# The first cross attention in four rounds a head instead of two, with SyncE's transfers laid out by quarters

## The reference, cut to what matters

```
q = qkv.reshape(bs * 16, ch, length)            # 16 heads, ch 16, length 512
k = v = y.reshape(bs * 16, ch, -1)              # 8192 keys
weight = einsum('bct,bcs->bts', q * scale, k * scale)
weight = softmax(weight.astype(float32), axis=-1)
a = einsum('bts,bcs->bct', weight, v)
x = x + a.reshape(bs, -1, length)
```

## Time and profile before

| | us |
|---|---|
| median of 3 runs (lowest, highest) | 1447.28 (1446.05, 1448.35) |
| the profiled execution, its own time | 1461.28 |
| its span, first to last instruction | 1459.5 |
| first cross attention in the span | 0 to about 701.8 |
| two negmax reductions in the steady part, one round apart | 297.53 and 317.35 |
| half clock in the stage, as granted in the trace | from 644.2 to 681.7 |
| mean granted TensorE clock | 0.982 |

### The profile page before, as it was taken

One profiled execution on the slowest core, in us unless ns is written; L12 is line 12 of the kernel. 1 busy time (PEld: TensorE's weight loads), 2 busy tenths in 40 slices (PEclk: granted clock), 3 DMA queues, 4 the chain that ended last, 5 costly groups with the idle time before them and its releaser, 6 DMA issues. The chain is left out here.

```text
span 1459.5 us, 27413 instructions
## 1 busy us (share of the span) xinstructions
PE 1398.2 (96%) x10740; PEld 847.7 (58%) x10740; DVE 1154.7 (79%) x1672; ACT 945.0 (65%) x1770; POOL 138.2 (9%) x171
## 2 busy tenths in 40 slices
PE   3999999999999999999899899999989889999998
PEld 2433333333333333333457899999978664568998
DVE  5999999999999999984587566666658447887665
ACT  1588888888888888876284455545533631785553
POOL 4122222212111222110000000000000000000000
PEclk9999999999999999986999999999999999999999
DMA  7644665554555444462204645554445523104540
GB/s 176 146 109 99 167 151 123 120 142 108 123 122 114 113 110 96 79 93 40 87 1 181 238 174 180 198 182 172 173 172 246 231 103 128 66 1 159 191 177 37
DMA packets 46338, 194.50 MB, mean 133 GB/s; under 512 B 16985, under 2 KB 17409, under 8 KB 34177
## 3 DMA queue, kind: packets, MB, share of 16 engines
q1 hardware_dynamic: 46032, 192.77, 44.9%
q10 hardware_dynamic: 192, 0.20, 0.1%
HBM read 167.69 MB, written 21.83 MB: 130 GB/s over the span
## 5 line engine op out<-in xcount | busy, mean ns | idle before, releaser
L526 DVE TENSOR_REDUCE pm<-bank 128x1 f32<-128x1024 f32 x512 | 621.2, 1221 | 24.6 <-PE bank L607 19.1
L585 ACT ACTIVATE probs<-bank 128x512 f32<-128x512 f32 x1024 | 554.6, 598 | 112.3 <-PE bank L626 105.1
L607 PE MATMUL bank<-kst,qst 48*128 48x512 f32 x1024 | 375.1, 457 | 22.1 <-DMA qst<-qsplit 20.4
L626 PE MATMUL bank<-qst,kst 52*128 52x512 f32 (+1 forms) x1024 | 378.6, 458 | 2.9 <-DMA qst<-nscratch 2.0
L643 PE MATMUL bank<-probs,vext 128*32 128x256 f32 x3968 | 324.8, 400 | 0.0
L626 PEld LDWEIGHTS bank<-qst,kst 52*128 52x128 f32 (+1 forms) x1024 | 155.0, 189 | 219.2 <-ACT probs L585 188.5
L1292 PE MATMUL bank<-e_xhi,e_hi 128*128 128x256 f32 (+1 forms) x784 | 223.5, 285 | 5.0 <-DVE e_lo L1227 4.5
L1292 PE MATMUL bank<-e_xhi,e_lo 128*128 128x256 f32 (+1 forms) x784 | 223.2, 285 | 0.0
L1292 PE MATMUL bank<-e_xlo,e_hi 128*128 128x256 f32 (+1 forms) x784 | 223.2, 285 | 0.0
L643 PEld LDWEIGHTS bank<-probs,vext 128*32 128x32 f32 x3968 | 79.0, 109 | 185.7 <-issue 96.3
L607 PEld LDWEIGHTS bank<-kst,qst 48*128 48x128 f32 x1024 | 151.5, 189 | 29.6 <-DMA qst<-qsplit 20.4
(11 more groups left out here) (220 smaller groups left out, 1521.0 us busy)
## 6 DMA issues: line engine op xcount, KB each, us to landing
raw<-wall SPq DMA_DIRECT2D x34, 1536.0 KB, 6.6
kst<-kscratch SPq DMA_DIRECT2D x192, 128.0 KB, 4.5
raw<-wall SPq DMA_DIRECT2D x10, 2304.0 KB, 8.5
kscratch<-ksplit SPq DMA_DIRECT2D x15, 1024.0 KB, 4.6
kraw<-ctx_rows SPq DMA_DIRECT2D x16, 512.0 KB, 6.3
vraw<-ctx_vt SPq DMA_DIRECT2D x16, 512.0 KB, 7.2
ctxT<-ctxT SPq DMA_DIRECT2D x8, 1024.0 KB, 11.6
nat<-ctx_chunks SPq DMA_DIRECT2D x6, 1024.0 KB, 21.6
```

What stands on the lines that cost most here:

```text
L526: nc.vector.tensor_reduce(pm[:, h % 2, r % 4, c:c + 1], bank[:, 2 * (r % 2):2 * (r % 2) + 2, :], AX.XY, ALU.max).then_inc(pre_reduced, 1)
L585: nc.scalar.activation(probs[:, (XST * k + n) % PR, :], bank[:, S_BANK[k][n], :], ACT.Exp, scale=XSCALE).then_inc(probs_ready, 1)
L607: ins = nc.tensor.matmul(bank[:, 2 * (r % 2) + j, :], qst[64 * j:64 * j + KR, h, tt * P:tt * P + P], kst[64 * j:64 * j + KR, h % 2, c * 51 ...
L626: nc.tensor.matmul(bank[:, S_BANK[k][n], :], kst[64 * j:64 * j + rows, h % 2, m * P:m * P + P], qst[64 * j:64 * j + rows, h, :], start=Tru ...
```

## The change

`NS` becomes 4: 64 rounds of 16 tiles, 8 iterations and 4 groups of values each. LAGP, FIRST_V and V_SCORE stay. The maximum of a round is the running one over the head's parts so far, so each round but the first of a head has a weight, three for a head instead of one. The total of a head is kept in `osb[:, 0]`: for every later round GpSimd multiplies it by the weight and adds the copied sum of the round. ScalarE copies after every round. SyncE's list is written anew for the four parts. The weights of the next stage come in eight transfers instead of four.

```
-NS = 2
+NS = 4
+W_AT = 2 * (XP + 4 - LAGP)
+    def later(k):
+        return k // NS * (NS - 1) + k % NS
 # SyncE (loads of the last heads left out)
+            for t in range(XN):
+                h, part = divmod(t, NS)
+                if t > 0:
+                    stack_negmax(t - 1)
+                if part == 0:
+                    if h < XH - 1:
+                        store_split(h + 1)
...
+                if part == 1:
+                    if h < XH - 1:
+                        load_stack(h + 1, 0)
...
+                    if 0 < h < XH - 3:
+                        sp.wait_ge(split_step, 2 * h + 4)
+                        load_raw(h + 3)
+                    if h > 0:
+                        sp.wait_ge(o_summed, (NS - 1) * h)
+                        sp.dma_start(oscratch[h - 1], osb[:, 1 + (h - 1) % 2, :]).then_inc(o_stored[(h - 1) % 2], 16)
+                if part == 2:
+                    if h < XH - 1:
+                        load_stack(h + 1, 1)
...
+                if part == 3:
+                    if h < XH - 1:
+                        load_q(h + 1)
...
+                    if h < XH - 2:
+                        sp.wait_ge(v_ready, h + 1)
+                        load_v(h + 2)
+                if t > 0 and (t - 1) % NS > 0:
+                    store_weight(t - 1)
+                    spread_weight(t - 1)
+
             stack_negmax(XN - 1)
             for h in range(XHA // 2, XHA):
                 load_nd(h)
+            store_weight(XN - 1)
+            spread_weight(XN - 1)
 # GpSimd
+            def weigh(k):
+                n = later(k)
+                pool.wait_ge(weight_moved, 32 * n)
+                if k % NS == 1:
+                    pool.wait_ge(o_copied, k)
+                else:
+                    pool.wait_ge(o_summed, n - 1)
+                total = osb[:, 0, :].rearrange("p (t c) -> p c t", t=4)
+                nc.gpsimd.tensor_tensor(total, total, weights[:, :, :], ALU.mult).then_inc(weighted, 1)
+            def sum_o(k):
+                h, part = divmod(k, NS)
+                pool.wait_ge(weighted, later(k))
+                pool.wait_ge(o_copied, k + 1)
+                to = osb[:, 0 if part < NS - 1 else 1 + h % 2, :]
+                nc.gpsimd.tensor_tensor(to, osb[:, 1 + h % 2, :], osb[:, 0, :], ALU.add).then_inc(o_summed, 1)
+            for k in range(XN):
+                h, part = divmod(k + 1, NS)
+                split_negmax(k)
+                if k % NS > 0:
+                    if later(k) > 2:
+                        pool.wait_ge(weight_ready, later(k) - 2)
+                    nc.gpsimd.tensor_tensor(mdiff[:, later(k) % 2, :], negmax[:, k % 4, :], negmax[:, (k - 1) % 4, :], ALU.subtract).then_inc(apart, 1)
+                if k > 0 and (k - 1) % NS > 0:
+                    weigh(k - 1)
+                    sum_o(k - 1)
+                if part == 1 and h < XH - 2:
                     split(h + 2)
+                if part == 1 and h == XH - 1:
                     ...   # the two memsets of nd
+                if part == 2 and h < XH - 1:
                     values(h + 1)
 # ScalarE: copy_o(k) after every round; the weight
+                    if n == W_AT and (k + 1) % NS > 0:
+                        act.wait_ge(apart, later(k + 1))
+                        if later(k + 1) > 1:
+                            act.wait_ge(weight_moved, 32 * (later(k + 1) - 1))
 # TensorE: pre waits for the keys of a head's first half in part 0, of the second half in part 2
-            for part of w_attn0: one transfer of 1024 KB
+            for part and half of w_attn0: one transfer of 512 KB
```

More of the change, by code:

```diff
@@ L315, in load_stack @@
                 if h >= 2:
-                    sp.wait_ge(scores, XST * (NS * (h - 2) + half + 1))
+                    sp.wait_ge(scores, XST * (NS * (h - 2) + NS // 2 * (half + 1)))
                 for rows in K_ROWS:
@@ L363, in _ @@
             sp.wait_ge(qsplit_ready, 4)
[L365 to L409, removed]
@@ L449, in _ @@
             nc.gpsimd.memset(marks[:, :, :].bitcast(F32), 1.0).then_inc(const_set, 1)
-            pool.wait_ge(const_set, 1)
-            nc.gpsimd.memset(marks[0:2, 1, :].bitcast(F32), 0.0).then_inc(const_set, 1)
+            for part in range(1, NS):
+                pool.wait_ge(const_set, part)
+                nc.gpsimd.memset(marks[0:2 * part, part, :].bitcast(F32), 0.0).then_inc(const_set, 1)
             nc.gpsimd.tensor_copy(g.identb[:, :], ident[:, :]).then_inc(g.ident_ready, 1)
@@ L467, in split_negmax @@
                                         ALU.subtract).then_inc(nsplit_step, 1)
[L469 to L480, removed]
@@ L482, in _ @@
-            for h in range(XH):
-                split_negmax(NS * h)
-                if h < XH - 2:
+            def weigh(k):
+                n = later(k)
+                pool.wait_ge(weight_moved, 32 * n)
+                if k % NS == 1:
+                    pool.wait_ge(o_copied, k)
+                else:
+                    pool.wait_ge(o_summed, n - 1)
+                total = osb[:, 0, :].rearrange("p (t c) -> p c t", t=4)
+                nc.gpsimd.tensor_tensor(total, total, weights[:, :, :], ALU.mult).then_inc(weighted, 1)
@@ L491, in _ @@
                     pool.wait_ge(nd_set, 2)
[L492 to L495, removed]
+                if part == 2 and h < XH - 1:
                     values(h + 1)
-                split_negmax(NS * h + 1)
-                nc.gpsimd.tensor_tensor(mdiff[:, h % 2, :], negmax[:, (NS * h + 1) % 4, :], negmax[:, NS * h % 4, :], ALU.subtract).then_inc(apart, 1)
-            weigh(XH - 1)
+            weigh(XN - 1)
         @block.vector
@@ L524, in _ @@
                     dve.wait_ge(pre_scores, XP * k + r + 1)
-                    c = 4 * half + r // 4
+                    c = 8 // NS * half + r // 4
                     nc.vector.tensor_reduce(pm[:, h % 2, r % 4, c:c + 1], bank[:, 2 * (r % 2):2 * (r % 2) + 2, :],
@@ L529, in _ @@
                 if k >= 4:
-                    dve.wait_ge(apart, (k - 4) // NS + 1)
-                nc.vector.tensor_reduce(negmax[:, k % 4, :], pm[:, h % 2, :, 0:4 * half + 4], AX.X, ALU.max, negate=True).then_inc(negmax_ready, 1)
+                    dve.wait_ge(apart, later(k - 3))
+                nc.vector.tensor_reduce(negmax[:, k % 4, :], pm[:, h % 2, :, 0:8 // NS * (half + 1)], AX.X, ALU.max, negate=True).then_inc(negmax_ready, 1)
             turn_negmax(XN - 1)
@@ L560, in copy_o @@
             def copy_o(k):
-                h, half = divmod(k, NS)
+                h, part = divmod(k, NS)
                 act.wait_ge(pv_done, XG * (k + 1))
-                if half == 0 and h > 0:
-                    act.wait_ge(o_summed, h)
-                if half == 1 and h >= 2:
+                if part == 0 and h > 0:
+                    act.wait_ge(o_summed, (NS - 1) * h)
+                if part == 1 and h >= 2:
                     act.wait_ge(o_stored[h % 2], h // 2 * 16)
-                nc.scalar.copy(osb[:, 0 if half == 0 else 1 + h % 2, :], bank[:, V_BANK[k], :]).then_inc(o_copied, 1)
+                if part > 1:
+                    act.wait_ge(o_summed, later(k) - 1)
+                nc.scalar.copy(osb[:, 0 if part == 0 else 1 + h % 2, :], bank[:, V_BANK[k], :]).then_inc(o_copied, 1)
             act.wait_ge(g.ident_ready, 2)
@@ L588, in _ @@
                         copy_o(k - 1)
[L589 to L593, removed]
+                    if n == W_AT and (k + 1) % NS > 0:
+                        act.wait_ge(apart, later(k + 1))
+                        if later(k + 1) > 1:
+                            act.wait_ge(weight_moved, 32 * (later(k + 1) - 1))
+                        nc.scalar.activation(weight[:, :], mdiff[:, later(k + 1) % 2, :], ACT.Exp, scale=XSCALE).then_inc(weight_ready, 1)
             copy_o(XN - 1)
@@ L664, in late_values @@
             def late_values(k, i):
[L665 to L669, removed]
+                k, n = divmod(XP * k + i - FIRST_V, XP)
+                if k >= 0:
+                    pv(k, n // 2, n % 2)
             def keep_busy(times):
@@ L698, in _ @@
                     first_busy(3)
-            pe.wait_ge(const_set, 4)
+            pe.wait_ge(const_set, NS + 2)
             for k in range(XN - 1):
@@ L1709, in perceiver, with loads_a @@
         cb1 = at(0, "cb1", [P, E1, T])
-        def loads_a(sp, part):
-            sp.dma_start(w_attn0[:, part], ins["w_attn0"][:, part]).then_inc(w_attn0_loaded, 16)
-            if part:
+        def loads_a(sp, part, half):
+            deep = slice(DC // 2 * half, DC // 2 * half + DC // 2)
+            sp.dma_start(w_attn0[:, part, deep], ins["w_attn0"][:, part, deep]).then_inc(w_attn0_loaded, 16)
+            if part or half:
                 return
```

86 lines of the change are left out of this document (61 added, 25 removed).

## The result

The changed kernel takes 1866.36 us (median of 4 runs, 1862.17 to 1877.11) against 1447.82 us before: 1.290 times as long, 95% interval 1.285 to 1.294. (Of the four runs before, three took 1446.05 to 1448.35 us and one 4515.4 us; the median of all four is given.) Its profiled execution took 1865.39 us, 404 us more than that of before, all in the first stage, which ends near 1107 us instead of 701.8.

A forecast was written before the change was run, and what follows sets the result against it. TensorE and VectorE bound the loop; 60 loops at half clock (1036.8 us) plus stalls of 60.8, 75.6 and 2.9 us, with start and tail, end the stage 569 us later: 2030 us profiled, 2025 us taken, range 1640 to 2080.

The forecast's parts named there:

- the likeliest case: Whole kernel: half clock in nearly the whole loop, about 2025 us, range 1960 to 2080, chance 0.72.
- the second case: TensorE's clock held or regained after stalls: 1648 us from stalls alone, 1730 to 1815 with short falls; chance 0.15.
- the signs: Changed profile: VectorE, GpSimd and TensorE waits, clock at 0.50 until the last round, negmax of parts 2 and 3 17.3 us apart.
- The 8.2 us of the last round: End of the stage: half of the last round goes, 16 exponentials at 0.51 us, saving 8.2 us.
- GpSimd's queue: Add ahead of split_negmax: 45 late rounds, stalls of 2.9 or 6.3 us at full clock, 1.96 or 5.4 at half.
- the rival "GpSimd's lateness hides": At VectorE's turn: 1.5 us of slack hides GpSimd's lateness; 1439 us, not slower 0.08, or slower for load_q 0.05.
- load_q: SyncE, part 3: queries land 2.1 us late per head, 31 us over 15 heads at full clock, none in a slow loop.
- The weights at "zero, at most 1 us a head": SyncE's three weight transfers a head end some microseconds before ScalarE and GpSimd want them: zero, at most 1 us a head.
- The prediction's rivals near 1439 and 1470 us: GpSimd's lateness hidden: 1439 us with load_q hidden too (not slower, 0.08), 1470 with load_q late and clock held (0.05).
- The clock: TensorE in the loop: falls to 1.2 GHz from the first late rounds to the last round, 2.16 us an iteration, not 1.239.
- The tail: From the last negmax to the stage's end: 34 us, where before it took 38.1.
- the prediction's first alternative: Profiled to timed scale: timed runs may lack the dip, then nothing of the 14 us comes off; otherwise 20 us do.

The follow-up runs named there:

- e1: The changed kernel with GpSimd's add of a round's sum moved behind the split, nothing else: 1631.22 us, 1.130 times before.
- e10: Four-part kernel, add behind split, bulk transfers spread evenly and issued ahead of each part's weight, GpSimd's split in the second part: 1612.32 us, 1.109 times before.
- e3: The kernel before with seven idle memsets (about 3.7 us) ahead of GpSimd's split in rounds 3 to 31: 1813.68 us median, one run 1689.74.
- e2: The changed kernel with the add behind the split, load_q moved to part 2 and the sum's store from part 1 to 2: 1593.60 us, 1.101 times before.
- e7: The changed kernel with weights stored and spread right behind the maxima's transfers and load_q in part 1, GpSimd's queue unaltered: 1874.11 us, 1.294 times before.
- e6: The changed kernel with the add behind the split, weights stored and spread right behind the maxima's transfers, load_q in part 1: 1591.91 us, 1.096 times before.
- e4: The kernel before with seven idle memsets ahead of GpSimd's split in round 12 alone: 1454.71 us, ratio 1.0045.
- e5: The kernel before with three of the six loads of nd moved behind the last head's maxima: 1446.83 us, ratio 0.9997.
- e9: Four-part kernel with the add behind the split and weights first, without the key loads of heads 2 to 15 (work left out): 1487.72 us, ratio 1.029.

## Why the prediction was right, and where its size was off
**How right.** The measured 1866 us lie in the range of 1640 to 2080, and the mechanism, GpSimd's add ahead of the split, is the one that was named. But the likeliest case had a range of its own, 1960 to 2080, and the time is not in it; it is in the whole range because that was stretched down over the second case. Of the signs, the waits of VectorE, GpSimd and TensorE came as told. The clock did not stay at 0.50, and so the negmax of part 2 and part 3 stand 10.1 to 14.9 us apart and not 17.3. From part 1 to part 2 it is 20.3 to 22.9 us (22.7), and 17.2 in head 14, which has no split in that place.

**What bounds.** Right: VectorE and TensorE had no room, and no round was made up for later.

**Savings and additions.** The 32 reductions and copies cost nothing that e1 to e10 could show apart. The 8.2 us of the last round were never seen, since every version lost more elsewhere; no run shows them.

**GpSimd's queue.** Right in place and in count: 46 late turns (45 in the loop and the last round's), and TensorE idle before L648 45 times, 14 of them long and 31 short. The total, 138.9 us, is near the 136 of 45 rounds at half clock (1.96 and 5.4 us), but this is in part luck. 33 of the 45 waits began at full clock, where the prediction's prices were 2.9 and 6.3 us; they took about 2.35 and 5.75. Those at half clock, or just after it, took 1.0 to 1.4 and 4.4 to 4.8. With the right clock for each wait, the prediction's prices would have made some 170. e3 shows that this lateness by itself costs 243 us or more, and e1 that without it 235 us go. In both, the stall and the clock are not parted. The 1.5 us of slack that the rival "GpSimd's lateness hides" starts from does not come out of its rows: 320.25 - (318.70 + 1.18) is 0.37 us, as the sum itself had it, so this rival was weaker still than it was put.

**SyncE.** load_q: right in kind. In the changed kernel it was seen 3 times (4.7 us), as the prediction had it for a slow loop; in e1, at a quicker pace, 13 times. The weights at "zero, at most 1 us a head" were wrong as a statement on the design: once the split is on time ScalarE waits for them about once a head, 4.9 us in the mean and up to 9.4 (e2). In the changed kernel itself this costs nothing (e7). The prediction's rivals near 1439 and 1470 us assumed that nothing else stood behind GpSimd, and e1, e2 and e6 refute that: 1592 to 1631 us.

**The clock.** The term of the sum that was mis-sized. The prediction had the loop at 2.16 us an iteration from round 3 to the end, because the mix had not brought the clock back in 20 us. It does bring it back: within 7 us in e4, and in the changed kernel 39 times from 60 to 1076 us, after 6.8 to 37.5 us at 0.50, 13.7 in the median and 625 in all. One such stretch, and what follows it:
```profile
345.24:362.31 17.07, 16.93 (x95) 5.62 (x95) 8.73 (x9) 8.77 (x17) 1.30 (x2) 0.50 0.24 79
362.31:365.70 3.39, 1.96 (x18) 0.65 (x14) 2.62 (x4) 1.18 (x3) 2.12 (x4) 1.00 0.03 5
```
Against the 1036.8 + 139 = 1176 us predicted for the 60 loops from round 3, they took 1006 us (negmax at 69.68 and 1076.07):
```profile
69.68 0.19 DVE L568 TENSOR_REDUCE negmax<-pm 128x4 f32<-128x32 f32 x1
...
1076.07 0.19 DVE L568 TENSOR_REDUCE negmax<-pm 128x4 f32<-128x32 f32 x1
```
At full clock and without stalls they would be 60 x 9.91 = 595 us. Of the 412 us more, about 140 are stalls and the rest, about 270, is put down to the clock; the prediction had 139 and 442. The 170 us between are more than the whole of 2025 - 1866 = 159. Against them stands the beginning, which took 9 us more than predicted (the negmax of round 3 at 69.68 us, not 60.6): the clock was at 0.50 from 41.5 to 55.2 us, and the prediction had these rounds at full clock. Rows 10 were one piece of 20 us; a price for 1000 us was drawn from it. The likeliest case, half clock in nearly the whole loop, and its rival, a clock that comes back, were both off, and the time lies between them.

By the Trainium skill, "TensorE: Matmul & The Clock Gate", section "What's actually happening", activity releases the throttle. e4 agrees with it, since TensorE was busy for all of the 6.8 us before the clock was back; in rows 10 and in e3 it was busy for 19.46 of 19.80 us and for 26.21 of 27.30 us, and the clock stayed at 0.50. What differs between them, the traces do not say.

**The tail.** 34 us predicted from the last negmax to the end of the stage; it took 31 (1107.2 - 1076.1). TensorE's last sum waited 4.4 us for GpSimd's weigh. The median of before lacks the dip (e5), so nothing of the 14 us was to be taken off, as the prediction's first alternative said; it took 5.

## What to carry to other kernels
When a loop's period is halved, write down for each queue in order when each instruction's input comes, counted from the start of the period: what came within a period before may come after the next one has begun, and then everything urgent behind it is late (here an add that waits for a copy at 11.8 us, with a period that went from 19.8 to 9.9). A queue that is busy 19% of the time, as GpSimd was, can be the bound. And count each stall of TensorE at its idle time plus what the clock takes after it, read from more than one place of the trace.

## What the runs showed of the hardware that was not expected
- Repeated stalls cost more than one. One stall of 2.80 us made its round 6.2 us longer (e4); the same stall in every round cost 8.4 us each in the lowest run and 12.7 in the median, and 14.3 us a round in the trace, with 27.3 us of 34.1 at half clock (e3).
- The length of a stall alone does not tell whether the clock falls. It fell after 1.51 us idle in the trace of before (644.0 us) and stayed at 1.00 after 1.78 us idle in that of e4 (650.9 us), both in the last head and both for the rows of the maxima:
```profile
650.94 0.50 PE L632 MATMUL bank<-qst,kst 50*128 50x512 f32 x1 [1.78 <-DMA qst<-nscratch]
```
- The same program with these stalls ran in 1813 to 1831 us three times and in 1690 us once (e3). Why was not found.
- The load that waits for a store of 16 KB comes 1.4 us after it when nothing was issued in the 5 us before (the median of 6 rounds of e6_weights_first), and 1.6 to 9.4 us after it, 3.8 in the median, behind 1 MB or more issued in these 5 us (29 rounds). The amount alone does not settle it. Without the key loads the waits of TensorE that follow fall from 28 to 10 (e9).
